# Layer 1 of a four-layer graph network: a third buffer for the bf16 parts and the residual add on GpSimd; layer 2: the epilogue one key tile earlier

## What is computed

```python
# layer 0 and 3: graph attention, e = leaky_relu(s1[i] + s2[j]), softmax over the neighbours
# layer 1: channel attention
feat = softplus(x * (INV_SQRT2 * w0) + b0)
scores = feat * wa + ba
attn = softmax(where(mask[i, j], scores[j, d], -1e9), axis=j)
out = einsum('bijd,bjd->bid', attn, feat)
# layer 2: four heads h_k = x Wh_k, then one output unit on leaky_relu(concat) Wo
scores = einsum('nd,md->nm', h, h)             # within a unit
attn = softmax(where(mask, scores, -1e16))
out = attn @ h + b                             # then leaky_relu; the output unit adds a layernorm
```

## Time and profile before

| what | us |
|---|---|
| median of 3 runs (1998.01 to 2004.02) | 2002.39 |
| the profiled execution, whole | 2003.45 |
| its span, first to last instruction | 2001.6 |
| PE busy in the span (95%) | 1906.4 |
| DVE busy (84%) | 1681.5 |
| ACT busy (62%) | 1242.2 |
| POOL busy (50%) | 1008.6 |
| stretch of layer 1, its first product to its last | 230.8 to 421.4 |
| stretch of layer 2 | 421.5 to about 1785 |

### The profile page before, as it was taken

One profiled execution on the slowest core, in us unless ns is written; L12 is line 12 of the kernel. 1 busy time (PEld: TensorE's weight loads), 2 busy tenths in 40 slices (PEclk: granted clock), 3 DMA queues, 4 the chain that ended last, 5 costly groups with the idle time before them and its releaser, 6 DMA issues.

```text
span 2001.6 us, 95064 instructions
## 1 busy us (share of the span) xinstructions
PE 1906.4 (95%) x43624; PEld 1566.2 (78%) x43624; DVE 1681.5 (84%) x1991; ACT 1242.2 (62%) x1886; POOL 1008.6 (50%) x726
## 2 busy tenths in 40 slices
PE   7998898989999999999999999999999999989998
PEld 6787798977777777777777777777777777767887
DVE  6999988767788888888888888888888888867998
ACT  5887655436666666666666666666666666654342
POOL 6676866412354455445454454455435455354653
PEclk8999999999999999999999999999999999999999
DMA  7000000011111111111111111111111111101111
GB/s 182 4 4 4 2 2 2 2 25 33 34 34 35 34 35 34 35 34 31 36 29 32 35 34 35 34 35 34 35 32 29 36 31 34 35 13 25 25 25 35
DMA packets 88255, 61.24 MB, mean 31 GB/s; under 512 B 45616, under 2 KB 86832, under 8 KB 87856
## 3 DMA queue, kind: packets, MB, share of 16 engines
q1 hardware_dynamic: 85632, 54.57, 11.2%
q10 hardware_dynamic: 2224, 0.59, 0.1%
HBM read 8.98 MB, written 4.19 MB: 7 GB/s over the span
## 4 chain that ended last, share of the span: by engine, by line
PE 70%; DVE 14%; ACT 6%; POOL 5%; issue 2%; DMA 1%; SPq 1%; ACTq 0%; POOLq 0%; DVEq 0%
PE ACC L1632 30%; PE S L1813 23%; PE S L1792 6%; DVE ring L1406 5%; PE AX L1856 3%; DVE ring L1259 2%; PE AX L1865 2%; PE AX L1833 2%; POOL sp_log L782 1%; POOL ln_sq L785 1%; ACT ring L1059 1%; DMA FA<-lo 1%; PE AX L1612 1%; DVE ch_rden L1391 1%; ACT st_x L898 1%
## 5 line engine op out<-in xcount | busy, mean ns | idle before, releaser
L1632 PEld LDWEIGHTS ACC<-V,ring 128*64 128x64 f32 x28672 | 955.4, 138 | 179.6 <-DVE ring L1259 34.6
L1406 DVE TENSOR_TENSOR ring<-ring,mask_self_t 128x1024 f32<-128x1024 f32 x640 | 896.0, 1410 | 193.2 <-ACT ring L1059 188.8
L1632 PE MATMUL ACC<-V,ring 128*64 128x65 f32 x28672 | 974.0, 223 | 29.1 <-ACT accs L870 11.9
L1059 ACT ACTIVATE ring<-S,dot_bias 128x1024 f32<-128x1024 f32 x640 | 713.7, 1116 | 414.1 <-PE S L1813 376.0
L1813 PE MATMUL S<-FA 128*64 128x512 f16 x5120 | 666.0, 382 | 4.7 <-DMA FA<-lo 4.6
L1813 PEld LDWEIGHTS S<-FA 128*64 128x64 f16 x5120 | 253.7, 110 | 164.7 <-ACT ring L1059 16.0
L1259 DVE SCALAR_TENSOR_TENSOR ring<-S,pair_q,mask_t 128x1024 f32<-128x1024 f32 x256 | 315.2, 1273 | 15.4 <-DVE f_max L1271 4.6
L798 POOL TENSOR_TENSOR EV_both<-score,recip 128x512 f32<-128x512 f32 x64 | 124.3, 1942 | 323.2 <-DVE score L1415 323.1
L1792 PE MATMUL S<-parts,mask_t 128*128 128x128 bf16 x3072 | 176.1, 221 | 10.8 <-DVE X L1395 10.6
L1792 PEld LDWEIGHTS S<-parts,mask_t 128*128 128x128 bf16 x3072 | 175.0, 99 | 11.8 <-issue 11.8
L791 POOL TENSOR_TENSOR V<-v_pairs,bh_bc 128x512 f32<-128x512 f32 x64 | 95.5, 1493 | 120.8 <-ACT v_pairs L1079 120.8
(11 more groups left out here) (134 smaller groups left out, 2044.2 us busy)
## 6 DMA issues: line engine op xcount, KB each, us to landing
FA<-hi SPq DMA_DIRECT2D x320, 64.0 KB, 2.0
FA<-lo SPq DMA_DIRECT2D x320, 64.0 KB, 2.0
X<-in_x SPq DMA_DIRECT2D x16, 256.0 KB, 5.0
ring<-in_adj SPq DMA_DIRECT2D x8, 512.0 KB, 8.1
out_x<-X SPq DMA_DIRECT2D x16, 256.0 KB, 2.6
wh<-in_wh_t ACTq DMA_DIRECT2D x2, 64.0 KB, 6.5
bh_bc<-in_bh ACTq DMA_DIRECT2D x1, 128.0 KB, 9.4
w_gat<-in_w_gat ACTq DMA_DIRECT2D x4, 16.0 KB, 3.8
```

The costliest lines, as they stand in the source:

```text
L1059: act.activation(ring[:, jt, :], S[jt % 2][:, :], ACT.Exp, bias=dot_bias[:, n % 2:n % 2 + 1])\
L1406: dve.tensor_tensor(ring[:, jt, :], ring[:, jt, :], mask_self_t[:, jt, :], ALU.mult)\
L1632: last = pe.matmul(acc_of(t)[rows, :], ring[:, jt, t * P + c * CUT:t * P + (c + 1) * CUT], values, start=(jt == 0 and t % 4 == 0), stop=(j ...
```

## The change

Layer 1: `parts` gets a third buffer (batch b in buffer b % 3), and ScalarE's first part of batch b waits for product b-3 instead of b-2. VectorE no longer adds to X; GpSimd does so in `channel_add(k-2)`, in step k after the score, and once more after the last step. TensorE waits for `o` (`ch_o`) instead of `x_done[1]`, and VectorE's result of batch b waits for GpSimd's add of batch b-1 before it may write `o` again. Layer 2: `epilogue` moves from jt 3, behind `feature_rest`, to jt 2.

```diff
-        parts = sb("parts", [P, 2, 3, T, 2 * D], BF16)
+        parts = sb("parts", [P, 3, 3, T, 2 * D], BF16)
...
+            def channel_add(b):
+                if exists(b):
+                    pool.wait_ge(ch_o, b + 1)
+                    pool.tensor_tensor(x_of(b), x_of(b), tiles(o[:, :]), ALU.add).then_inc(x_done[1], 1)
+
             def channel_step(k, par):
                 if k > 0:
                     channel_score(k, par)
+                channel_add(k - 2)
                 channel_norm(k, par)
...
             channel_layer(channel_step, first_norm, lambda: values(UNITS[0]))
+            channel_add(B - 1)
...
-                    wait(act, ch_full, b - 1)
-                    act.activation(parts[:, 1 - par, 0], EV[:, :, :], ACT.Copy).then_inc(ch_p1, 1)
+                    wait(act, ch_full, b - 2)
+                    act.activation(parts[:, b % 3, 0], EV[:, :, :], ACT.Copy).then_inc(ch_p1, 1)
...
             def channel_result(k, par):
                 b = k - 1
                 if exists(b):
-                    wait(dve, x_done[0], B)
+                    dve.wait_ge(x_done[0], B)
+                    wait(dve, x_done[1], b)
...
-                    dve.wait_ge(ch_o, b + 1)
-                    dve.tensor_tensor(x_of(b), x_of(b), tiles(o[:, :]), ALU.add).then_inc(x_done[1], 1)
...
+                if jt == 2 and 0 < u["n"] < LAST["n"]:
+                    epilogue(UNITS[u["n"] - 1])
                 if jt == 3 and nxt:
                     feature_rest(nxt)
-                if jt == 3 and 0 < u["n"] < LAST["n"]:
-                    epilogue(UNITS[u["n"] - 1])
...
                 pe.wait_ge(ch_p3, k + 1)
-                wait(pe, x_done[1], k - 1)
+                wait(pe, ch_o, k - 1)
...
                 if m < 2:
-                    pe.wait_ge(x_done[1], B - 1 + jt)
+                    pe.wait_ge(ch_o, B - 1 + jt)
```

More of the change, by code:

```diff
@@ L1037, in channel_exponent @@
                     act.wait_ge(ch_r1, b + 1)
-                    act.activation(parts[:, 1 - par, 1], EV_rest[:, :, :], ACT.Copy).then_inc(ch_p2, 1)
+                    act.activation(parts[:, b % 3, 1], EV_rest[:, :, :], ACT.Copy).then_inc(ch_p2, 1)
                 b = k + 2
@@ L1367, in channel_part @@
                     wait(dve, ch_p3, b)
-                    dve.tensor_tensor(EV_rest[:, :, :], EV[:, :, :], parts[:, 1 - par, 0], ALU.subtract)\
+                    dve.tensor_tensor(EV_rest[:, :, :], EV[:, :, :], parts[:, b % 3, 0], ALU.subtract)\
                         .then_inc(ch_r1, 1)
@@ L1381, in channel_part @@
                     dve.wait_ge(ch_p2, b + 1)
-                    dve.tensor_tensor(parts[:, 1 - par, 2], EV_rest[:, :, :], parts[:, 1 - par, 1], ALU.subtract)\
+                    dve.tensor_tensor(parts[:, b % 3, 2], EV_rest[:, :, :], parts[:, b % 3, 1], ALU.subtract)\
                         .then_inc(ch_p3, 1)
@@ L1792, in channel_step @@
                             last = pe.matmul(S[par][:, t * P:(t + 1) * P], mask_t[:, j, t * P:(t + 1) * P],
-                                             parts[:, par, part, j, :], start=(j == 0 and part == 0),
+                                             parts[:, k % 3, part, j, :], start=(j == 0 and part == 0),
                                              stop=(j == T - 1 and part == 2))
```

## The result

| | before | changed |
|---|---|---|
| median, us | 2002.77 (1998.01 to 2004.02, 12 runs) | 1997.32 (1995.5 to 1998.85, 12 runs) |
| ratio, 95% interval | | 0.9975 [0.9967, 0.9984] |
| span of the profiled execution, us | 2001.6 | 1995.1 |

The kernel became 0.25% faster: 5.4 us by the medians, 6.5 us by the two profiled executions. The time lies in the predicted range, but the forecast was a balance, and this is a small gain outside the noise of 12 runs. (The change adds 6 or 7 lines: L1798 after is L1792 before, L1839 is L1833, L1819 is L1813, L1445 is L1439, L797 is L791.)

What follows compares the result with a forecast made beforehand. Layer 1 was taken as bound by turns between TensorE and VectorE, layer 2 by TensorE with VectorE close behind; -11.7 + 8 + 4.6 - 0.6 = +0.3 us gave 2002.7 us from the 2002.39 median, range 1992 to 2011.

Steps and rivals of the forecast that it cites:

- Layer 1: TensorE's stalls between products in layer 1 and at its end: the change saves 11.7 us in all.
- The split: Layer 1's saving: 1.3 us first stall, 8.0 later stalls, 1.7 low clock, 0.7 end of stage.
- The five stalls: Layer 1, TensorE's stalls after the one at product 2: the third parts buffer removes all 8.0 us.
- Rival 3: Layer 1: VectorE becomes the bound at 11.2 us a step, 5 of 8.0 us stay, 2007.7 us; chance 0.09.
- The loss at L1375: Layer 1, VectorE's product beside GpSimd's add to X (L1368 before the change): it loses 0.8 us.
- the one on the output units: Layer 2 output units, b = 2 to 14: `lo` lands 1.67 us later, 5 to 18 us lost, 8 taken.
- The collision that was priced: Output units: GpSimd's square delays the leaky product, then `values` precedes mask product 3, making `lo` 1.67 us later.
- the forecast balance of +0.3: Whole kernel: -11.7 + 8 + 4.6 - 0.6 = +0.3 us against the profiled 2003.45 us.
- rival 1: Layer 2: mask product 3 gets ahead of `values`, output units keep their reserve, only head 3 pays: 1994.7 us; chance 0.27.
- Head 3: Layer 2: GpSimd's division delays the `stat_var` scaling, 0.35 us in 13 units, 4.6 us; first head 3 -0.6.

Runs made afterwards that it cites:

- the changed kernel with the statistics first: Changed kernel, but in heads 3 the epilogue's two rows stand behind the two statistics rows of jt 2: 1991.73 us, ratio 0.9951.

## Why the prediction was wrong, and where it held

**Layer 1 held, and was a little small.** One stall of 1.4 us at product 2, the clock behind it at 1.00, the products' end at 408.1 where some 410 was said: each as written. The split also held: 1.3 at the first stall, 1.6 by the clock behind it (product 2 took 12.3 us there, not the 12.5 that was read), 0.7 at the end of the stage (4.0 to 3.3 us of waiting ahead of L1862). The five stalls gave 8.8 instead of 8.0, since a restart costs 0.15 us more than the wait that the timeline shows. That makes 12.4 for the predicted 11.7.

The traces show 12.9, but the rest is an accident of two executions. Product 15 took 12.5 us before and 10.9 after, 1.6 less, by a low clock that lay over it. It is not the change that took it away, as the same product shows with layer 1 as before (the epilogue alone) and with layer 1 as changed (the epilogue late in output units). Before, then these two:

```profile
408.94 12.51 PE L1792 MATMUL S<-parts,mask_t 128*128 128x128 bf16 x192
```

```profile
409.97 10.88 PE L1792 MATMUL S<-parts,mask_t 128*128 128x128 bf16 x192
```

```profile
398.47 12.51 PE L1800 MATMUL S<-parts,mask_t 128*128 128x128 bf16 x192
```

In all other profiles of this study it took 10.88. Some 1.2 of the 1.6 are lost again right behind, in the first unit of layer 2 (19.54 us from its first dots to the next unit's, where 19.07 before less those 0.7 was due). That unit varies too: the same rows took 18.50 with layer 1 alone.

**Rival 3 was wrong at its bound.** VectorE's step was put at 10.3 to 11.2 us and took 9.92, below both bounds. The loss at L1375 came as worked out (0.7 for 0.8). But the step of the kernel before contained a scaling held up for 0.8 us (0.96, where 0.17 is its time alone) and a small wait, which went when GpSimd's rows shifted. The bounds counted what the add would newly disturb and only touched on what it would cease to disturb.

**The step that failed is the one on the output units.** "GpSimd is in the square of `stat_center` until 706.59" was read from the trace of before and taken as fixed, while the same edit was worked out against it. But the edit also acts in head 1, one unit ahead, where the prediction gave it a 0, since `lo` doesn't move there. It doesn't; VectorE's queue behind it does, by 0.8 us, and GpSimd's chain hangs on that. The collision that was priced never took place; the one that did costs less, 3.7 us in place of 8. With the epilogue kept late in head 1, the priced collision appears with its rows, and the kernel takes 2005.3 us. The rows of the collision were right and its price of 8 somewhat small (some 11); that it would occur was wrong. This term is 4.3 of the 5.3 us between the forecast balance of +0.3 and the -5.0 of the runs; layer 1 is 0.7 of the rest. That the time still lies in the range is luck: the range reached down there for rival 1, whose mechanism did not occur.

**Head 3 held to the hundredth**: 0.35 us in each of 13 units, by the mechanism named, and -0.6 in the first.

**Rival 1** (nothing lost in the output units) named the right direction and the wrong way: `values` didn't fall behind mask product 3 but ahead of the leaky product, and the units lost 3.7 us, not nothing.

**The rest, 1.0 us at the start of layer 3, isn't the change's either.** The clock over the first tiles behind the long wait there, before and then after:

```profile
1768.60:1777.50 8.90, 8.85 (x136) 6.29 (x138) 1.97 (x4) 3.38 (x5) 2.08 (x2) 0.67 0.01 2
```

```profile
1762.90:1771.80 8.90, 8.81 (x160) 6.58 (x162) 2.89 (x6) 4.29 (x5) 2.12 (x3) 0.78 0.01 2
```

At half clock for 5.9 us in one and 3.9 us in the other, while the wait ahead of it is nearly the same (5.16 and 5.00). From the first dots of the last head 3 to those of the last output unit it is 60.9 us before and 59.8 after. The kernel with the epilogue alone has 59.8 as well, the one with layer 1 alone 59.4 behind the same 5.16 us wait as before, and the changed kernel with the statistics first 60.7. So it follows neither half of the change. What sets where the low clock falls stays open.

The Trainium skill (SBUF — State Buffer, Who interferes with whom) says that a VectorE instruction with two SBUF inputs and a GpSimd instruction that reads SBUF contend, and that the one issued first keeps the other out. By that rule the order of arrival decides the cost, and the runs agree: the centring took 1.04 us when it was ahead of the mask product by 0.66 us, and 2.02 when it was behind by 0.15; the leaky product ended 0.54 us behind `values` in the changed kernel and 0.55 behind the square with head 1 late. The section also counts `tensor_scalar` among the operations that can take the shared ports, though it has one input; the 128x8 scaling was held up (0.52 against 0.17).

## What to carry to other kernels

An edit in a repeated order acts in every kind of unit, and the engines' phases at one place are set in the unit ahead: before pricing a collision from the old trace, follow the edit through the preceding unit on each engine that takes part, also where nobody waits. Where two engines exclude each other, 0.8 us of lead can be worth 8 us in a kernel, in either direction, so such a term needs both outcomes in the range. And a wait that repeats once a round is a queue that can be read row by row: moving what the waiter doesn't need behind what it does brought 18 us here, three times what the whole change brought.

## What the runs showed of the hardware

A stall of 2.7 us in layer 1 was followed by a granted clock of 0.86 over the next product; with 1.4 us in the changed kernel it stayed at 1.00. The same went for every other profile here: two more with the 2.7 us stall had the low clock behind it, ten more with 1.4 us did not. A low clock also lay over product 15 in two of the fourteen profiles, with the same 3.9 us of short pieces and waits ahead of it in all. So the length of a stall alone didn't decide it there.

Lockout between VectorE and GpSimd reached the smallest rows: 0.8 us on a scaling of eight columns in layer 1 before the change, and 0.35 us in each head 3 after it. A short row just behind one that releases GpSimd is a bad place; moved two rows up it cost nothing.
